# Loads by two queues, a moved bounds search, and score rows read from PSUM, in a four-network graph kernel

## The reference

```python
h = jnp.maximum(_layernorm(x, axis=-1), 0.0)
x = x + _L0_gnn_ref(h, edge_index, ...)      # attention, 4 heads of 512, then 1 head of 768
h = jnp.maximum(_layernorm(x, axis=-1), 0.0)
x = x + _L1_gnn_ref(h, edge_index, ...)      # the same with other weights
h = jnp.maximum(_layernorm(x, axis=-1), 0.0)
x = x + _L2_gnn_ref(h, node_type_3, edge_index, edge_type_3, ...)   # three relational layers
h = jnp.maximum(_layernorm(x, axis=-1), 0.0)
x = x + _L3_gnn_ref(h, edge_index, ...)      # attention, 8 heads of 96, then 1 head of 768
```

```python
h = (x @ W).reshape(N, heads, d_out)
as_n = jnp.einsum('nhd,hd->nh', h, a_src)
ad_n = jnp.einsum('nhd,hd->nh', h, a_dst)
e = jax.nn.leaky_relu(as_n[src] + ad_n[dst], 0.2)
ex = jnp.exp(e - segment_max(e, dst)[dst])
alpha = ex / (segment_sum(ex, dst)[dst] + 1e-16)
out = segment_sum(alpha[:, :, None] * h[src], dst)
```

## Time and profile before

| | |
|---|---|
| median of 3 runs | 1710.71 us |
| the profiled execution | 1716.61 us, its span 1714.8 us |
| PE busy | 1527.1 us, 89% of the span |
| DVE busy | 838.7 us, 49% |
| ACT busy | 594.2 us, 35% |
| POOL busy | 530.6 us, 31% |
| chain that ended last | PE 62%, DVE 13%, issue 9%, ACT 5%, DMA 5%, POOL 4% |
| DMA | 105.50 MB, mean 62 GB/s |
| mean granted clock of TensorE | 0.943 of full speed |

### The profile page before, as it was taken

One profiled execution on the slowest core, in us unless ns is written; L12 is line 12 of the kernel. 1 busy time (PEld: TensorE's weight loads), 2 busy tenths in 40 slices (PEclk: granted clock), 3 DMA queues, 4 the chain that ended last, 5 costly groups with the idle time before them and its releaser, 6 DMA issues.

```text
span 1714.8 us, 26856 instructions
## 1 busy us (share of the span) xinstructions
PE 1527.1 (89%) x10079; PEld 1475.4 (86%) x10079; DVE 838.7 (49%) x2119; ACT 594.2 (35%) x1183; POOL 530.6 (31%) x675
## 2 busy tenths in 40 slices
PE   4988899998879999986999999999999998867787
PEld 3758889997879889986999999999999998757787
DVE  6786776316467763255623323142231315489843
ACT  3334444223345542232322232222223121257721
POOL 3234233233233242233223232323235131133222
PEclk9978999999889999988899999999999999868898
DMA  2222111122211111232112122212133222101122
GB/s 92 86 76 58 36 45 44 54 77 90 77 49 42 38 46 53 64 110 95 36 33 57 53 58 60 55 57 62 37 86 83 85 73 91 46 22 35 35 73 92
DMA packets 88989, 105.50 MB, mean 62 GB/s; under 512 B 9689, under 2 KB 80840, under 8 KB 88861
## 3 DMA queue, kind: packets, MB, share of 16 engines
q1 hardware_dynamic: 72850, 75.06, 15.4%
q10 hardware_dynamic: 16011, 28.73, 5.2%
HBM read 88.12 MB, written 11.78 MB: 58 GB/s over the span
## 4 chain that ended last, share of the span: by engine, by line
PE 62%; DVE 13%; issue 9%; ACT 5%; DMA 5%; POOL 4%; DVEq 1%; ACTq 0%; POOLq 0%
PE ps L862 36%; PE ps L1066 7%; PE ps L958 5%; PE ps L1048 4%; DVE junk L1944 3%; DMA xl<-x_scratch 2%; DVE prob L1995 2%; PE ps L915 2%; PE ps L1110 2%; PE ps L1087 2%; DMA xl<-in_x 1%; DVE prob L2003 1%; POOL pairs L1202 1%; PE ps L885 1%; DMA x_first<-in_x 1%
## 5 line engine op out<-in xcount | busy, mean ns | idle before, releaser
L1202 POOL TENSOR_TENSOR pairs<-stage,pairs 128x256 fp32r<-128x256 f32 (+2 forms) x466 | 367.7, 807 | 786.0 <-ACT pairs L1291 784.9
L862 PE MATMUL ps<-pairs,XB 128*125 128x256 f32 (+2 forms) x2760 | 407.3, 309 | 23.8 <-issue 10.4
L862 PEld LDWEIGHTS ps<-pairs,XB 128*125 128x125 f32 (+1 forms) x2760 | 396.1, 195 | 27.5 <-issue 11.7
L862 PE MATMUL ps<-pairs,XA 128*125 128x256 f32 (+3 forms) x2505 | 356.4, 303 | 6.4 <-DVE XA L1624 2.3
L1291 ACT ACTIVATE pairs<-stage 128x256 fp32r<-128x256 f32 (+2 forms) x466 | 185.1, 423 | 499.3 <-PE ps L862 376.0
L862 PEld LDWEIGHTS ps<-pairs,XA 128*125 128x125 f32 (+1 forms) x2505 | 350.5, 187 | 8.4 <-issue 2.8
L1624 DVE TENSOR_TENSOR Hl<-ps,Hl 125x768 fp32r<-125x768 f32 (+3 forms) x57 | 43.6, 818 | 270.2 <-ACT Hl L1343 270.2
L958 PE MATMUL ps<-AT,Hg 125*128 125x314 f32 (+1 forms) x1080 | 167.5, 315 | 3.8 <-DVE rl L2032 3.8
L958 PEld LDWEIGHTS ps<-AT,Hg 125*128 125x128 f32 (+1 forms) x1080 | 162.4, 191 | 4.8 <-DVE rl L2032 3.7
L1249 POOL TENSOR_SCALAR prob<-prob,rden 125x625 f32<-125x625 f32 x80 | 78.1, 977 | 214.4 <-DVE rden L2011 214.4
L915 PE MATMUL ps<-ident,prob 125*125 125x125 f32 x475 | 86.1, 324 | 44.1 <-POOL prob L1249 18.8
(11 more groups left out here) (225 smaller groups left out, 1685.2 us busy)
## 6 DMA issues: line engine op xcount, KB each, us to landing
stage<-in_W SPq DMA_DIRECT2D x210, 128.0 KB, 2.3
stage<-in_rel SPq DMA_DIRECT2D x99, 192.0 KB, 2.4
stage<-in_root SPq DMA_DIRECT2D x91, 64.0 KB, 1.9
x_scratch<-xo ACTq DMA_DIRECT2D x15, 375.0 KB
xl<-x_scratch ACTq DMA_DIRECT2D x15, 375.0 KB
stage<-in_rel SPq DMA_DIRECT2D x42, 128.0 KB, 2.1
stage<-in_root SPq DMA_DIRECT2D x12, 192.0 KB, 2.4
stage<-in_W SPq DMA_DIRECT2D x12, 192.0 KB, 2.5
```

What stands on the lines that cost most here:

```text
L862: last = mm(o, X[:rows, xi, a, P * (s0 + t):P * (s0 + t) + m], pair(n, b), start=k == 0 and i == 0 and t * pitch % BANK == 0, stop=k == le ...
L1202: nc.gpsimd.tensor_tensor(pair(n, 1), staged(n), pair(n, 0).bitcast(F32), ALU.subtract).then_inc(*up("weights_lo", "weights lo", n))
```

## The change

Four things are changed. x's row tiles 0, 2 and 4 are loaded by ACT's queue and 1 and 3 by SP's, tile 1 between the first and second weight tile and tile 3 behind the third. The step `bounds_rest` moves behind the low halves of the whole input and behind one K tile. Two K tiles stand ahead of the windows instead of one, so the last stands behind window 9. In the three single heads the copy of the spread scores times 1 is left out: DVE's mask rows read the scores in PSUM, and the spread's two banks are held by PE until the step of mask rows 4 and are free when mask rows 4 are written.

```diff
+X_BY_ACT = (0, 2, 4)
...
+        yield from k_tile()
+        yield ("bounds_rest",)
         yield from k_tile()
         yield ("count", -1)
...
     for d in range(2, NT):
         yield ("load_x", d)
-    yield ("bounds_rest",)
...
+        def direct(l, h):
+
+            return h == GAT_HEADS[l][0]
...
                     q = acquire(*s)
+                    if direct(*s[1:]):
+                        held.update((place[q], place[q] + 1))
                     pe.wait_ge(*at("scores col", *s[1:]))
...
+                elif kind == "mask_rows":
+
+                    if direct(*s[1:3]) and s[3] == NT - 1:
+                        first_bank = place[fill_of["spread", *s[1:3]]]
+                        held.difference_update((first_bank, first_bank + 1))
...
+            def first_x(d):
+                sp.dma_start(x_first[:, d], I["x"][P * d:P * d + P, :]).then_inc(
+                    *up(f"x_first{d}", "x in", d, by=16))
...
+                    if n == 1:
+                        first_x(1)
                     if n == FIRST_TILES:
-                        sp.wait_ge(*at("x in", NT - 1))
+                        first_x(3)
+                        sp.wait_ge(*at("x in", 3))
+                        sp.wait_ge(*at("x in", 4))
...
-            for d in range(NT):
+            for d in X_BY_ACT:
                 act.dma_start(x_first[:, d], I["x"][P * d:P * d + P, :]).then_inc(
...
-                    for i, scale in enumerate((1.0, SLOPE)):
+                    for i, scale in list(enumerate((1.0, SLOPE)))[int(direct(l, h)):]:
...
-                    G.same(("scores", n, 1), "free", fill_of["spread", l, h])
+                    if not direct(l, h):
+                        G.same(("scores", n, 1), "free", fill_of["spread", l, h])
...
-                    V.scalar_tensor_tensor(out=prob[:, d, :N + 1], in0=asb[:, 0, :N + 1],
-                                           scalar=ad8[:, heads_order[l, h] % 2, d:d + 1], in1=asb[:, 1, :N + 1],
-                                           op0=ALU.add, op1=ALU.max).then_inc(*up("leaky_rows", "leaky rows", n))
+                    target = ad8[:, heads_order[l, h] % 2, d:d + 1]
+                    if direct(l, h):
+                        V.scalar_tensor_tensor(out=prob[:, d, :N].rearrange("p (j c) -> p j c", j=NT),
+                                               in0=pitched(fill_of["spread", l, h]), scalar=target,
+                                               in1=asb[:, 1, :N].rearrange("p (j c) -> p j c", j=NT),
+                                               op0=ALU.add, op1=ALU.max).then_inc(*up("leaky_rows", "leaky rows", n))
+                        if d == NT - 1:
+                            G.same(("leaky rows", n), "free", fill_of["spread", l, h])
```

More of the change, by code:

```diff
@@ L1994, in _ @@
                         dve.wait_ge(*at("mask", l == 3, d))
-                    V.scalar_tensor_tensor(out=prob[:, d, :N + 1], in0=asb[:, 0, :N + 1],
-                                           scalar=ad8[:, heads_order[l, h] % 2, d:d + 1], in1=asb[:, 1, :N + 1],
-                                           op0=ALU.add, op1=ALU.max).then_inc(*up("leaky_rows", "leaky rows", n))
+                    target = ad8[:, heads_order[l, h] % 2, d:d + 1]
[6 more added lines that the diff above has]
+                            G.same(("leaky rows", n), "free", fill_of["spread", l, h])
+                    else:
+                        V.scalar_tensor_tensor(out=prob[:, d, :N + 1], in0=asb[:, 0, :N + 1], scalar=target,
+                                               in1=asb[:, 1, :N + 1],
+                                               op0=ALU.add, op1=ALU.max).then_inc(*up("leaky_rows", "leaky rows", n))
                 elif kind == "score_rows":
```

## The result

The changed kernel takes 1726.40 us at the median of four runs (1724.78 to 1727.25); the kernel before, run beside it, 1710.40 us (1705.45 to 1710.97). The ratio is 1.0086 with an interval of 1.0062 to 1.0109; times 1711 us that is 14.7 us slower (10.6 to 18.7). The forecast was +4.5 us, with a range that ended at 1718.8. The direction was right and the size was not.

The account below looks back on a forecast made before the run. PE was taken to bound most of the program, with DVE setting the pace from 65 to 75 us. Start-up +0.7 and single heads +3.8 made +4.5 us: 1710.7 + 4.5 = 1715.2 us, range 1710.5 to 1718.8.

Parts of the forecast that it names:

- x by two queues: Start-up: no added bandwidth; row tiles 3 and 4 land together near 20.7 us, everything behind 1.2 us later.
- The step that failed: Start-up, moved search: ends at 36.1 us, first one-hot rows about 39.4, first count 1.4 us late.
- The step's second half: Windows after start-up: the 1.4 us reach window 5; the saved K tile falls where PE waits for DVE.
- The single heads: Networks 0, 1 and 3: spread banks held until mask rows 4 cost 1.5, 0.3 and 2.0 us, +3.8 together.
- The lateness of the third transposes: Single heads of networks 0 and 3: PE's third transpose waits for mask rows 4, 2.0 us later in each.
- The relief from PSUM sources: Single heads: mask rows reading PSUM take the normal 0.87 us, not up to 2.43 as beside a POOL addition.
- The fixed term of the Trainium skill: Mask rows: 120 cycles for PSUM against 58 for SBUF, 0.3 us more per head; the forecast counted 0.
- The bound of +1.1 on the start-up: Upper bound of the start-up term, forecast at +0.7 us with bounds -0.9 to +1.1.

Follow-up runs that it names:

- two_tiles: Kernel before with a second K tile ahead of the counts, search in its old place: 1717.41 us, ratio 1.0038.
- after_banks: Changed kernel with two PSUM banks skipped once, at the first transpose of network 1's input: 1723.28 us, ratio 1.0068.
- the skip: Two PSUM banks passed over once at the first transpose of network 1's input; with two_tiles, against the kernel before: 1713.09 us, ratio 1.0013.
- the second profile: Kernel before, unchanged, run and profiled once more: 1712.54 us, span 1710.7.
- search_only: Kernel before with the search of the bounds behind the low halves and a second K tile ahead of the counts: 1720.64 us, ratio 1.0058.
- hold_only: Kernel before, copies and SBUF reading kept, with the single heads' spread banks held until mask rows 4: 1716.35 us, ratio 1.0057.
- heads_only: Kernel before with only the single heads' edit, mask rows reading the scores in PSUM: 1716.05 us, ratio 1.0026.
- after_loads6: Changed kernel with PE loading six registers ahead of counts 0, 5 and 10, not sixteen ahead of count 0: 1725.34 us, ratio 1.0085.
- two_tiles_banks: Kernel before with two K tiles ahead of the counts and two PSUM banks skipped at network 1's first transpose: 1713.09 us, ratio 1.0013.
- x_only: Kernel before with only x's five row tiles loaded by two queues: 1713.68 us against 1711.46, ratio 1.0016.

## Why the prediction was wrong

**x by two queues: right.** Tiles 3 and 4 landed together, and the last statistics began at 21.96 us, where the earlier trace rows and the forecast's 1.2 us put them:

```profile
20.79 1.02 DVE L1631 BATCH_NORM_STATS2 bns<-x_first 125x6 f32<-125x384 f32 x2 [2.26 <-DMA x_first<-in_x]
...
21.96 0.97 DVE L1631 BATCH_NORM_STATS2 bns<-x_first 125x6 f32<-125x384 f32 x2
```

The low halves ended at 30.93 (30.8 forecast), and two K tiles at 36.52 (36.8).

**The step that failed** is "DVE's register loads took 3.2 us, so the first one-hot rows come at about 39.4 ... I take 1.4 us late". Count 0 came 7.2 us late. Three things are in it:
- The search was priced at 5.3 us, as in a place where POOL split no weights. POOL's first four splits stood at 31.04 to 33.8 us before, and the new place of the search is right beside them. Measured: 8.0, of which POOL makes 2.6.
- PE's own register loads were left out: the step has PE wait for the one-hot rows "alone". The chain of the kernel before shows 2.58 us of these loads (under two_tiles). They are 6.2 us, and what had hidden the other 3.6 was that the bounds were known before the K tile was issued. Behind a wait for the bounds, all 6.2 are on the path.
- DVE's ten loads are 3.87 us with nothing in front, against 3.21 in the earlier trace rows, for the same reason; but PE's are done later and decide.

The lower clock isn't among them, since count 0 had it before too. Only the K tile behind count 0 took 2.92 us and not 2.39. The slowing beside POOL could have been read from the kernel before, where an operation of the one-hot columns takes 0.72 us beside POOL's fifth split and its neighbour 0.25:

```profile
35.66 0.25 DVE L1856 TENSOR_SCALAR dsts<-iota,edgef 125x125 f16<-125x125 f16 x1
...
36.12 0.72 DVE L1856 TENSOR_SCALAR dsts<-iota,edgef 125x125 f16<-125x125 f16 x1
```

```profile
35.87 0.91 POOL L1202 TENSOR_TENSOR pairs<-stage,pairs 128x256 fp32r<-128x256 f32 x1 [2.05 <-ACT pairs L1291]
```

The step's second half, that the saved K tile does little, held: of 7.2 us 7.0 stand ahead of network 0's single head (5.3 in after_banks, the same program up to there).

**The term that wasn't there: the rotation of banks.** The prediction looked for new bank waits only behind the spread. But a K tile ahead of a count puts the tiles of PSUM that follow in other banks, and 600 us on, project2 of network 1 waits for DVE's products on a bank that before had been free long since: +4.0 us in the changed kernel's profile, 4.3 by the times of two_tiles with and without the skip.

**The single heads: the mechanism right, the size low.** Third transposes of networks 0 and 3 wait 2.33 us for mask rows 4, as said. The first additions began at 413.15, 758.16 and 1693.96 us, 9.6, 13.8 and 10.9 later than in the earlier trace rows, where the heads had begun 6.6, 12.5 and 8.1 late: 3.0, 1.3 and 2.8 us, a sum of 7.1 against 3.8. The lateness of the third transposes was sized right, 2.1 us in both networks. What was missing is that the output behind runs at the lower clock for longer: 7.79, 7.62 and 7.12 us, where before it took 6.4. PE's windows in network 0, of the changed kernel and then of the kernel before:

```profile
405.20:409.00 3.80, 3.80 (x14) 0.50 0.33 109
409.00:413.00 4.00, 4.00 (x21) 0.84 0.12 47
```

```profile
396.50:400.00 3.50, 3.50 (x16) 0.71 0.34 135
400.00:403.00 3.00, 3.00 (x19) 1.00 0.31 124
```

Behind network 1's head 2.5 to 2.9 us of a delay are given back (between 758 and 771 us of the second profile, in search_only and two_tiles too), so the edit alone costs 4.4 by the times. That this is near the 3.8 is luck in part: the three heads were sized too low, and the giving back was not in the sum. The relief from PSUM sources was right: no mask rows of the single heads took over 869 ns. The fixed term of the Trainium skill ("VectorE: DVE Perf Modes", The TRN2 errata) is not to be seen in them (min/median/max ns):

```profile
L2019 DVE SCALAR_TENSOR_TENSOR prob<-ps,ad,asb x15: 860/867/869, 396.1 to 1684.7; 125x625 f32<-125x625 f32 x15
```

**The sum** by the runs: search moved 6.3, second K tile 2.2, rotation 4.3, heads 4.4, x 0.4 to 2.7, which is 17.6 to 19.9 against 14.7 (10.6 to 18.7) for the whole; with search, tile and rotation taken together, as search_only measured them (9.9), it is 14.7 to 17.0. The bound of +1.1 on the start-up was no bound: it varied what the sum had in it, and none of what it had left out.

What stays open: whether x's edit costs more than its 1.3 us at the start, since the times say 0.5 to 5.0, why hold_only is slower than heads_only, and what differs between 410 and 630 us from one execution to the next.

## What to carry to other kernels

- A gap called "issue" ahead of an instruction can be the part of sequencer work that isn't hidden. Before you put a wait in front of such loads, count them and price each one from a place where nothing hides it.
- When work is moved in time, read what the other engines do at its new place: small operations of VectorE took 0.65 us beside GpSimd's in place of 0.17.
- Where buffers are handed out in turn, one more request early on changes every later neighbour. Compare who had each buffer last over the whole program, and not only around the edit.

## What the runs showed of the hardware

- With nothing beside them, 16 register loads took 6.18 us on PE and 6 took 3.04 (after_loads6); 10 took 3.87 on VectorE. Worked out from the two on PE, that is 0.31 us a load and, as an estimate, 1.2 us for a group however small.
- In the kernel before, PE's sequencer had run ahead of all 15 matmuls of a K tile when the first began; with 30 in front it reached the loads 2.7 us behind the first, in two_tiles and in two_tiles_banks (6.18 us back from 41.16 and 40.39). So 2.8 to 3.6 us of the loads were hidden. The Trainium skill ("Perfetto Trace Analysis", Per-engine timelines) says that it goes on to the next instruction once it has pushed one into the wait queue; how deep that is, the runs alone show.
- The granted clock was 1.2 GHz (0.50) from 45 to 50 us behind 8 idle us. In the kernel before, behind 2.58 idle us, the same 14 matmuls took the same 3.85 us, against the 1.00 in its clock column there; x_only, with the same 2.58 idle us, had 1.00 to 40.6 us, then 0.50, and took 2.85. A clock column is worth checking against the time of like matmuls.
- Operations of VectorE on 18 numbers took 0.65 us beside GpSimd's of 128x256 (0.70 us each) and 0.17 without them.
